# An edge network on one core: two tiles of edges in 32 filled by single-column copies instead of gathers

## The reference

```
h = relu(layernorm(x));  x = x + relu((sum over edges of norm * h[col]) @ W0.T + b0)
h = relu(layernorm(x))
z = relu([h[src], h[dst], edge_feat] @ W1 + b1)      # 112 -> 128
z = relu(z @ W2 + b2)                                # 128 -> 128
x = x + (mean over the edges of each dst of (z @ W3 + b3))
```

## Time and profile before

| | us |
|---|---|
| median of 3 runs | 7111.28 (7111.13 to 7126.65) |
| span of the profiled execution | 6161.4 |
| median above that span | 949.9 |
| edge stage, first to last gather | 2192.0 to 6108.2 |

### The profile page before, as it was taken

The page is one execution under the profiler, slowest core; times in us unless marked ns, Lnnn a source line. Parts: engine busy times, 40 slices in busy tenths (PEclk is TensorE's granted clock), DMA queues, the critical chain, the costliest instruction groups (busy, mean ns, idle before and its releaser), DMA issues. The chain is left out here.

```text
span 6161.4 us, 148527 instructions
## 1 busy us (share of the span) xinstructions
PE 5105.3 (83%) x40298; PEld 4259.0 (69%) x40299; DVE 3550.1 (58%) x11415; ACT 1709.0 (28%) x3091; POOL 4073.1 (66%) x3903
## 2 busy tenths in 40 slices
PE   4885999999999768778888877787787888888877
PEld 4883899999999656666666666666666666666666
DVE  8998999999996643443434434434344343434444
ACT  3336666666663321111111111111111111111110
POOL 0106667666664467777777777777777777777776
PEclk9998999999999888888888888888988888888888
DMA  9206999999999733333333333333333333333332
GB/s 165 32 0 161 278 289 288 288 291 290 290 291 271 177 107 83 83 85 83 85 83 83 85 84 83 85 83 84 84 83 85 83 84 84 84 84 84 83 85 66
DMA packets 653787, 816.43 MB, mean 133 GB/s; under 512 B 426282, under 2 KB 471052, under 8 KB 653114
## 3 DMA queue, kind: packets, MB, share of 16 engines
q1 hardware_dynamic: 478251, 592.65, 32.8%
q0 software_dynamic: 175360, 221.63, 17.0%
HBM read 563.36 MB, written 250.47 MB: 132 GB/s over the span
## 5 line engine op out<-in xcount | busy, mean ns | idle before, releaser
L1729 POOL DMA_INDIRECT p_got<-p_tab,idx_d x3128 | 2962.5, 947 | 964.4 <-issue 864.2
L1715 ACT ACTIVATE h<-z,b_col 128x512 f32<-128x512 f32 x782 | 537.6, 687 | 3391.9 <-PE z L1855 3343.6
L1719 DVE TENSOR_TENSOR h<-z,nb 128x512 f32<-128x512 f32 x782 | 540.9, 692 | 1606.3 <-PE z L1695 1598.6
L1689 PEld LDWEIGHTS z<-ident_f,p_got 128*128 128x128 f32 x3128 | 415.8, 161 | 1385.5 <-DMA p_got<-p_tab,idx_d 1239.8
L1689 PE MATMUL z<-ident_f,p_got 128*128 128x128 f32 x3128 | 596.9, 323 | 784.9 <-DMA p_got<-p_tab,idx_d 784.7
L1073 PE MATMUL a_ps<-tile_r,pair_l 128*128 128x288 fp8e5 x5280 | 1041.4, 287 | 75.4 <-DVE tile_r L1160 45.5
L910 POOL DMA_INDIRECT sum_tab<-val_s,idx_s x496 | 788.9, 1590 | 466.9 <-ACT val_s L1027 332.5
L1094 PE MATMUL out_ps<-gw,a_got 121*128 121x144 bf16 x11340 | 1076.4, 225 | 4.5 <-DMA a_got<-a_tab 4.2
L1695 PEld LDWEIGHTS z<-w_sb,h 128*128 128x128 f32 x6256 | 1033.5, 234 | 56.4
L1695 PE MATMUL z<-w_sb,h 128*128 128x128 f32 x6256 | 1023.6, 318 | 0.0
L1036 ACT CAST stage<-a_ps 128x576 uint16<-128x576 f32 x1320 | 838.6, 640 | 405.0 <-PE a_ps L1073 397.4
(11 more groups left out here) (202 smaller groups left out, 3692.9 us busy)
## 6 DMA issues: line engine op xcount, KB each, us to landing
a_tab<-stage SPq DMA_DIRECT2D x330, 576.0 KB
a_got<-a_tab SPq DMA_DIRECT2D x330, 576.0 KB
rel<-rel_row SPq DMA_DIRECT2D x391, 192.0 KB
p_got<-p_tab,idx_d POOLq DMA_INDIRECT x3128
ef<-in_edge_t SPq DMA_DIRECT2D x391, 64.0 KB
q_win<-q_tab SPq DMA_DIRECT2D x782, 24.0 KB
src_bc<-src_row SPq DMA_DIRECT2D x124, 128.0 KB
a_tab<-big SPq DMA_DIRECT2D x22, 472.5 KB
```

What stands on the lines that cost most here:

```text
L1689: pe.matmul(out_tile, p_rows[:, j, :], ident_f[:, :], start=False, stop=False, is_transpose=True, skip_group_check=True)
L1729: pool.indirect_dma_start(p_rows[:, j, :], None, p_tab, bass.IndirectOffsetOnAxis(idx[:, j:j + 1], 0)).then_inc(landed, 16)
```

## The change: what it does

In slots 0 and 4 of every eight steps (`OWN`), from step 8 on, the last of the four tiles is not gathered. Two tiles in 32 are so treated. Instead:

- The node stage keeps all of h, turned, in `h_all` (48 partitions by 12672 nodes), in `big`: one more ScalarE copy for each of its 14 pieces. `seg_acc` becomes a tile of its own, which ScalarE and VectorE clear at the start of the edge stage, a half each, in place of GpSimd.
- An early stage writes the source nodes of these tiles, 16 bit each, to a small table `own_row`; it takes one ScalarE copy, transpositions on TensorE, a copy back and a store.
- SyncE loads one row of it (`own_idx`, 128 numbers on one partition) once for each such tile, after waiting until the tile before it in that buffer has been built.
- The 128 columns of a tile are built in four consecutive steps, a quarter in each, 16 by VectorE and 16 by ScalarE, into `h_col[b]`. As there are two such tiles in eight steps, every step builds one quarter. The quarters of the tile of slot 0 are built in slots 1 to 4, seven to four steps before its use.
- For its 16 columns an engine loads the node numbers in two loads of 8 registers (`LOT`), near the start of its step: VectorE before it adds the segment, ScalarE before it waits for z1. The copies come at the end of the step.
- TensorE, in such a step, turns three gathered tiles and multiplies the fourth's `h_col` by the source part of W1 (`w1a_sb`), once `cols_made` says that it is complete.
- VectorE loads the first node's number before it waits for the segment's sum, where it did so after that wait. The turning of counts works on 32 partitions from 64 on, as `cnt_acc` moves there.
- Several semaphores of the last stage are merged; its order of work stays.

```
+OWN = (0,4)
+OWN_TILE = GROUP - 1
+QUARTERS = 4
+LOT = 8
...
+                def building(q, s):
+
+                    for b, slot in enumerate(OWN):
+                        k = (s - slot - 1) % DEPTH
+                        after = DEPTH - 1 - k
+                        if k < QUARTERS and (not isinstance(q, int) or DEPTH <= q + after < NE):
+                            yield b, slot, k, after
+
+                def nodes_of(engine, b, first):
+
+                    return [nc.values_load_multi_w_load_instructions(
+                        own_idx[b][0:1, at:at + LOT], engines=[engine], min_val=0, max_val=N - 1,
+                        skip_runtime_bounds_check_because="they are the sources of edges, each below N")[1]
+                        for at in (first, first + LOT)]
+
+                def columns(copy, b, first, nodes):
+
+                    for lot in range(2):
+                        for i, node in enumerate(nodes[lot]):
+                            at = first + lot * LOT + i
+                            last = copy(h_col[b][0:F, at:at + 1], h_all[:, bass.ds(node, 1)])
+                        last.then_inc(cols_made[b], 1)
...
@@ scalar, the node stage
+                        wait_past(act, h_t_ready, 2 * (k - 2))
                         act.copy(h_t[0:F, :, :], t_ps_c[:, 0:CB, :]).then_inc(h_t_ready, 1)
+                        act.wait_ge(h_t_ready, 2 * (k - 2) + 1)
+                        act.copy(h_all[:, (k - 2) * CB * P:(k - 1) * CB * P],
+                                 h_t[0:F, :, :].rearrange("p c n -> p (c n)")).then_inc(h_t_ready, 1)
...
@@ gpsimd, the node stage
-                pool.wait_ge(agg_ready, NK)
-                pool.memset(seg_acc, 0.0).then_inc(t_zero, 1)
-                pool.wait_ge(t_zero, 4)
...
@@ sync, the edge stage, in a step
+                        for b, slot in enumerate(OWN):
+                            use = q + (DEPTH - 2)
+                            if s == (slot + 2) % DEPTH and (not isinstance(q, int) or DEPTH <= use < NE):
+                                sp.wait_ge(cols_made[b], (q + (DEPTH - 2 - slot)) * 2)
...
+                                sp.dma_start(own_idx[b][:, :], own_row[bass.ds(row, 1), :]).then_inc(own_loaded[b], 16)
...
@@ gpsimd, in a step
-                        gather(pool, p_got[s % UNROLL], half_of(idx[s // 2], s), gathered[s % UNROLL])
+                        gather(pool, p_got[s % UNROLL], half_of(idx[s // 2], s), gathered[s % UNROLL], gathered_tiles(q, s))
...
@@ scalar, in a step
+                        lots = []
+                        for b, slot, k, after in building(q, s):
+                            if k == 0:
+                                act.wait_ge(own_loaded[b], (q + (after - slot)) * 2)
+                                act.sem_inc(any_turn, 1)
+                            first = (2 * k + 1) * 2 * LOT
+                            lots.append((b, first, nodes_of(mybir.EngineType.Activation, b, first)))
                         act.wait_ge(z1_made, q + 1)
...
                         make_h1(act, h1[s % 2], z1[s % 2]).then_inc(h1_ready, 1)
-
+                        for b, first, nodes in lots:
+                            columns(act.copy, b, first, nodes)
...
@@ tensor, in a step
+                        src_part(pe, z1[k], p_got[s % UNROLL], gathered_tiles(q, s))
+                        if owned(q, s):
+                            b = OWN.index(s)
+                            pe.wait_ge(cols_made[b], (q + (COLS - s)) * 2)
+                            pe.sem_inc(pe_turns, 1)
+                            pe.matmul(each_tile(z1[k])[OWN_TILE], w1a_sb[:, :], h_col[b][:, :], start=False, stop=False,
+                                      skip_group_check=True)
...
@@ vector, in a step
                         if past(q, 1):
                             keep_h2(q - 1, (s - 1) % 2)
+                        lots = []
+                        for b, slot, k, after in building(q, s):
...
+                            first = 2 * k * 2 * LOT
+                            lots.append((b, first, nodes_of(mybir.EngineType.DVE, b, first)))
                         if past(q, 2):
                             add_segment(q - 2, (s - 2) % UNROLL)
+                        for b, first, nodes in lots:
+                            columns(dve.tensor_copy, b, first, nodes)
```

More of the change, by code:

```diff
@@ L201, in build_gnn @@
     src_row = dram("src_row", [SG, W], U16)
+    OWN_STEP = DEPTH // len(OWN)
+    OWNS = NG // OWN_STEP
+    assert OWN == tuple(range(0, DEPTH, OWN_STEP)) and OWN_STEP >= QUARTERS and P == QUARTERS * 4 * LOT
+    assert max(g for g in range(NE) if g % DEPTH in OWN) * GROUP + OWN_TILE < EDGES // P
+    own_row = dram("own_row", [OWNS, P], U16)
     g_tab = dram("g_tab", [NPP, PLANES * F], BF16)
@@ L636, in _ @@
                 for c in range(SG * GROUP // TURNED):
-                    last = pe.transpose(turned_ps[:, c, :], src_s[:, c * TURNED:(c + 1) * TURNED], ident_f[:, :])
+                    pe.transpose(turned_ps[:, c, :], src_s[:, c * TURNED:(c + 1) * TURNED], ident_f[:, :])
+                for c in range(OWNS // OWN_ROWS):
+                    last = pe.transpose(own_ps[:, c, :], own_f[:, c * OWN_ROWS:(c + 1) * OWN_ROWS], ident_f[:, :])
                 last.then_inc(turned, 1)
@@ L1684, in edge_part, with src_part @@
             return pe.matmul(z1[:, :], w1c_sb[:, :], ef, start=True, stop=False, skip_group_check=True)
[L1686 to L1689 removed]
+        def src_part(pe, z1, p_rows, tiles=range(GROUP)):
+            for j in tiles:
+                pe.matmul(each_tile(z1)[j], p_rows[:, j, :], ident_f[:, :], start=False, stop=False, is_transpose=True,
                           skip_group_check=True)
@@ L1722, in add_seg, with gather @@
         def add_seg(dve, first, seg_ps, nodes):
-            at, count = seg_acc[:, bass.ds(first, nodes)], cnt_acc[0:1, bass.ds(first, nodes)]
+            at, count = seg_acc[:, bass.ds(first, nodes)], cnt_acc[:, bass.ds(first, nodes)]
             dve.tensor_tensor(at, at, seg_ps[:, 0:nodes], ALU.add)
-            return dve.tensor_tensor(count, count, seg_ps[0:1, nodes:2 * nodes], ALU.add)
-        def gather(pool, p_rows, idx, landed):
-            for j in range(GROUP):
+            return dve.tensor_tensor(count, count, seg_ps[CNT_AT:CNT_AT + 1, nodes:2 * nodes], ALU.add)
+        def gather(pool, p_rows, idx, landed, tiles=range(GROUP)):
+            for j in tiles:
                 pool.indirect_dma_start(p_rows[:, j, :], None, p_tab, bass.IndirectOffsetOnAxis(idx[:, j:j + 1], 0)
                                         ).then_inc(landed, 16)
-        cnt_acc = sb("cnt_acc", [1, NPP], F32)
+        seg_acc = sb("seg_acc", [P, NPP], F32)
         with ExitStack() as life:
@@ L1785, in slot_count, with owned, gathered_tiles, rows_landed @@
                     return in_slot(q, s, DEPTH, per)
+                COLS = P // LOT // 2
+                SEG_CUT = NPP // 2
+                def owned(q, s):
+                    return s in OWN and past(q, DEPTH)
+                def gathered_tiles(q, s):
+                    return [j for j in range(GROUP) if j != OWN_TILE or not owned(q, s)]
+                def rows_landed(q, s):
+                    own = [slot in OWN for slot in range(s % UNROLL, DEPTH, UNROLL)]
+                    cycle = GROUP * len(own) - sum(own)
+                    before = s // UNROLL
+                    if isinstance(q, int) and q < DEPTH:
+                        return (before + 1) * GROUP * 16
+                    return (q - s) // DEPTH * (cycle * 16) + (GROUP * (before + 1) - sum(own[:before + 1]) + sum(own)) * 16                         if isinstance(q, int) else (q - s) * (cycle * 16 // DEPTH) + (
+                            GROUP * (before + 1) - sum(own[:before + 1]) + sum(own)) * 16
+                def building(q, s):
[15 more added lines that the diff above has]
+                        last.then_inc(cols_made[b], 1)
                 def half_of(pair, s):
@@ L1920, in _ @@
                     for s in range(UNROLL):
-                        last = dve.memset(cnt_col[s][:, :], 0.0)
+                        dve.memset(cnt_col[s][:, :], 0.0)
+                    for b in range(len(OWN)):
+                        last = dve.memset(h_col[b][:, :], 0.0)
                     last.then_inc(ef_zero, 1)
@@ L1924, in _ @@
                     hots(0, 0)
+                    dve.memset(seg_acc[:, 0:SEG_CUT], 0.0).then_inc(cnt_zero, 1)
                     def step(q, s):
```

96 lines of the change are left out of this document (61 added, 35 removed).

## The result

The changed kernel takes 8589.55 us (8580.43 to 8593.8), the kernel before, run beside it, 7112.31 us. The ratio is 1.2077 (1.2059 to 1.2095): 1477 us slower, where I had forecast 6901 us and a range that ended at 7520.

What follows compares the result with a forecast made beforehand. GpSimd's gathers were taken to bound the edge stage. From the span, 6161.4 - 243 + 9 + 5 + 3 + 1 + 15 = 5951 us; with 949.9 us carried over, 6901 us, range 6850 to 7520.

Steps and rivals of the forecast that it cites:

- Register loads: Edge stage, VectorE and ScalarE: two loads of eight node numbers a step, 0.35 us each, 0.70 us a step.
- the rival that pays for each value: Edge stage: two loads of 2.44 us make VectorE's step 8.8 us and the time 10080 us; chance 0.15.
- The sum of VectorE's stream: Edge stage: adds, five instructions, first-node load, 16 copies and two loads total 4.36 us, under the gathers' 4.70 us.
- my 0.25: Edge stage, VectorE's longer loop body: code fetching at 2 us a turn, 0.25 us a step.
- The step of 5.01 us: Edge stage of the kernel before: four gathers, one each 1.25 us on a full GpSimd, make the step.
- 949.9 us "carried over unchanged": Whole kernel: the median of the runs lies 949.9 us above the profiled span, and this was added unchanged.
- The rival by the 200 ns per register: Edge stage: loads of 3.2 us a step make VectorE's step 7.1 us, time near 8750 us; within greatly slower, 0.15.
- Gathers removed: Edge stage, GpSimd: 194 gathers left out, each worth its whole interval of 1.2524 us, 243 us less.
- Copies on ScalarE: Edge stage: 16 copies a step at 0.12 us, 1.9 us, fit in ScalarE's free time and cost nothing.
- Gathers slowed: Edge stage: VectorE's new copies beside the gathers lengthen each by 3 ns, 9 us in all.
- Around the loop: Outside the edge loop: 5 us for copies of h, 3 for clearing the sum, 1 for the identifiers at the start.
- It can't catch up: Edge stage: VectorE at 4.6 of 4.7 us can't catch up after a slow TensorE step, 15 us (0 to 60).

Runs made afterwards that it cites:

- the kernel with pairs: Changed kernel with one load of eight 32-bit words a step and engine, each word two node numbers taken apart in registers: 8265.23 us, ratio 1.157.
- the second profile of before: The kernel before, run again unchanged and profiled, with a span of 7080.2 us: 7102.93 us, ratio 0.9988.
- one tile in 64: Changed kernel with one tile in 64 built by copies, not two in 32: 7644.78 us, ratio 1.0702, with plain loads; 7544.99 us, 1.0552, with numbers in pairs.

## Why the prediction was wrong

**The step that failed** is "Register loads. [...] I take 0.35 us, because the row looks like one round trip". It measured 1.825 us, and two a step are 3.65 and not 0.70. My own last sentence named it ("wrong first if a load of eight takes over 0.6 us"). The one value that I knew cost 0.305 us and I took the seven others as free because the one hardly varies; a steady row says nothing of a second value. The rule that I set against it (the Trainium skill, Runtime: NRT & Kernel Launch, Instruction fetch mechanics: about 200 ns per register even in bulk) agrees with these loads of 16-bit numbers, 0.22 us each. It doesn't with the 32-bit words of the kernel with pairs, eight in 0.595 us. I gave the rival that pays for each value 0.15 of the chance. Of two bounds far apart I had taken the one that made the change worth while.

**The sum of VectorE's stream** was right but for the loads and the stops. With 3.65 in place of 0.70, my 4.36 becomes 7.31 us; the step is 8.0, and 0.7 is left. The 16 copies were even cheaper than I took them: 15 in 1.57 us are 0.10 us apart, not 0.125, which makes 1.1 us left over. So code and unevenness cost far more than my 0.25. Where nothing stops it the sum fits: the shortest slot has 7.1 us. The mean step is 0.9 us longer. 0.37 of them are the idle time behind the jump back, once in eight steps: 2.9 us (median), and 2.9 to 3.2 in all five kernels whose VectorE code is fetched, at most 0.4 in all others. I had taken 2 us a turn for all fetching. The rest are stops such as the 0.51 and 0.59 us of the timeline, which nothing explains. q14 carries 1050 packets, 10 more in each of some 94 turns than in the kernel before (91). The run without loads has 97 such packets and a VectorE body of 288 instructions, so the fetches come with the loads' code. These 0.9 us matter as much as the rest: by the sum alone, 7.1 us against 6.1, the change would have cost some 780 us and not 1477.

**The step of 5.01 us and the 949.9 us "carried over unchanged"** is the second failure, and it would have spoilt the number even with the right load. I took the difference between span and runs for something outside the program's work. Most of it was in the edge stage: a step of 6.1 us on most chips. The rival by the 200 ns per register of the Trainium skill's rule, 8750 us, came within 2% of the result by luck, two errors that cancel: 7.1 us a step instead of 8.0, and 5.0 instead of 6.1 before it. Set rightly, (8.0 - 6.1) x 782 = 1490 us, and 1477 were measured.

**Gathers removed**, 194 x 1.2524 = 243 us: 243 on the quicker chip, 266 on a slower one. The size was right, and what a gather is worth is the best-founded term of the prediction. That GpSimd is the bound was right too, in the sense that the time hangs on the gathers: leaving out TensorE's transposes gave 0.3% on a slower chip.

**Copies on ScalarE, "at nothing"**: right on the quicker chip (0.9605). **Gathers slowed**, 9 us: nothing, the median is 944 ns with the copies and 947 without. **Around the loop**, 9 us: the first gather starts at 2259.4 us, against 2256.9 in the second profile of before, so 2.5 us.

**"It can't catch up"**, 15 us: too small a term for what one tile in 64 showed, about 640 us with long steps in half of the slots, of which some 310 are stops among the copies.

**What the change could bring with free node numbers** differs by chip. On slower ones it is nothing: 266 us from the gathers and as much back through the copies, VectorE's above all. On the quicker one each engine's copies alone leave the gain whole, 4%; all copies together were not run there. No version that keeps all of the work beat the kernel before.

**Left open**: why TensorE's increments reach the others up to 10 us late on the slower chips (ScalarE's start behind the record of z1 has medians of 0.3 to 3.4 us in the profiles with steps of 4.8 to 6.8 us, that with ScalarE's own loads apart, and 0.04 in the two with 7.6 and 8.0), why ScalarE's and VectorE's copies are stopped there, and why copies on VectorE lengthen the step without filling it. That these go together is seen, a cause is not shown. The granted clock of TensorE is lower there as well, and whether that is a cause or follows from the waiting no run tells.

## What to carry to other kernels

Cost a register load by its values and their width: on VectorE 0.28 to 0.31 us for the first and 0.22 for each further one of 16 bit, but 0.6 us for eight words of 32 bit. None of it is in the busy column; look for it as "issue" before the next instruction. Where numbers must come from memory into registers to save a gather of 1.25 us, 128 of 16 bit are 16 x 1.825 = 29 us of an engine's stream.

Keep the loop body of each engine short enough not to be fetched: here one jump back into a fetched body cost VectorE some 3 us.

When a profile's span and the timed runs are 13% apart, nothing may be carried over as a constant: the stage that one edits may be another one in the timed runs. Run the unchanged kernel once more and read that profile first.

An engine that has room on the mean may have none in the step; add up the longest step too, not only the average one.

## What was not expected of the hardware

The same kernel takes 7100 to 7150 us on five chips and 6176 us on a sixth, with the same gathers (0.945 us long, 1.25 us apart within a burst) and a granted TensorE clock of 0.77 against 0.88 in the stage. On the slower ones TensorE's increments arrive in groups. The clearest case is the run without loads and nearly without copies, ScalarE's timeline:

```profile
4009.17 0.69 ACT L1740 ACTIVATE h<-z,b_col 128x512 f32<-128x512 f32 x1 [9.09 <-remote]
...
4009.93 0.68 ACT L1740 ACTIVATE h<-z,b_col 128x512 f32<-128x512 f32 x1
...
4021.35 0.69 ACT L1740 ACTIVATE h<-z,b_col 128x512 f32<-128x512 f32 x1 [10.56 <-remote]
...
4022.11 0.68 ACT L1740 ACTIVATE h<-z,b_col 128x512 f32<-128x512 f32 x1
```

Two steps 0.76 us apart, then 11.4 us of nothing. Two z1 cannot be 0.76 us of TensorE's work apart when one takes 3.3 us at the full clock; the increments have waited somewhere.

Code was fetched anew in each turn once the body of one engine's loop was long enough. These are the q14 rows of the runs with loads of one value, with loads of four and of the kernel with pairs:

```profile
q14 instruction: 97, 0.79, 0.0%
```

```profile
q14 instruction: 573, 4.69, 0.2%
```

```profile
q14 instruction: 1147, 9.40, 0.4%
```

The longest body of a turn is 297 instructions in the first (VectorE's), 345 in the second and 465 in the third, whose ScalarE has 357. The lowest that is fetched is 300, VectorE's with one tile in 64 and pairs (572 packets). Five to six packets of 8 KB a turn are fetched for each engine whose body has 300 or more, none for one of 297 or fewer; the bodies are counted as the records of one turn in the trace. The Trainium skill (Runtime: NRT & Kernel Launch, Instruction fetch mechanics) has two blocks of 256 instructions kept; here a body well under 512 is already fetched again. A body that begins inside a block could touch a third, which would fit, but no run here moves one.
